# Storing q and k once, copying shifted keys inside SBUF, and moving value rows with GpSimd

## What is computed

```python
qkv = x @ W_attn + b_attn
q, k, v = heads(split(qkv))                    # 16 heads, 16 channels each
scores = einsum('bhtd,bhsd->bhts', q, k) * scale
mask = causal & (j >= i - 64)                  # each token sees itself and the 64 before it
attn = softmax(where(mask, scores, -inf))
x = layernorm(x + (attn @ v).reshape(b, t, c) @ W_proj + b_proj)
expert_idx = argmax(softmax(x @ Wr.T))
inter = sum_e (expert_idx == e) * gelu(x @ W1[e] + b1[e])
out = layernorm(x + layernorm(inter @ Wo + bo + x) * gamma + beta)
```

## Time and profile before

| | |
|---|---|
| median of three runs | 532.12 us (528.19 to 534.21) |
| the profiled execution | 528.38 us, of which its span is 526.7 us |
| mean granted TensorE clock | 0.979 of full speed |
| share of the span busy | PE 93%, DVE 82%, ACT 68%, POOL 60% |
| bytes moved by DMA | 80.96 MB |

### The profile page before, as it was taken

One profiled execution on the slowest core, in us unless ns is written; L12 is line 12 of the kernel. 1 busy time (PEld: TensorE's weight loads), 2 busy tenths in 40 slices (PEclk: granted clock), 3 DMA queues, 4 the chain that ended last, 5 costly groups with the idle time before them and its releaser, 6 DMA issues. The chain is left out here.

```text
span 526.7 us, 24512 instructions
## 1 busy us (share of the span) xinstructions
PE 489.4 (93%) x8574; PEld 432.2 (82%) x8574; DVE 431.5 (82%) x1132; ACT 356.5 (68%) x796; POOL 315.4 (60%) x553
## 2 busy tenths in 40 slices
PE   6989999999999999899978898999999999999980
PEld 5878888788888888688866787888999989999970
DVE  6558798878987898669898567999999989999983
ACT  5677778777876878467867664566667757666860
POOL 8612446444464545434634347777888878888883
PEclk9999999999999999989999898999999999999996
DMA  8687688786977797768772122222235554442200
GB/s 200 165 245 198 185 220 205 204 217 180 259 211 213 196 255 197 188 191 222 174 205 72 44 61 62 71 64 63 77 105 183 206 182 162 163 147 71 53 25 7
DMA packets 90184, 80.96 MB, mean 154 GB/s; under 512 B 36502, under 2 KB 83871, under 8 KB 90018
## 3 DMA queue, kind: packets, MB, share of 16 engines
q1 hardware_dynamic: 86720, 70.95, 48.9%
q0 software_dynamic: 3248, 8.41, 4.7%
q10 hardware_dynamic: 98, 0.04, 0.0%
HBM read 43.50 MB, written 23.55 MB: 127 GB/s over the span
## 5 line engine op out<-in xcount | busy, mean ns | idle before, releaser
L1415 PE MATMUL ps<-v_even,w_hi 128*128 128x128 f16 x1024 | 142.1, 220 | 0.6 <-issue 0.3
L1397 PE MATMUL ps<-wo_hi,ks 128*128 128x256 f16 (+1 forms) x576 | 129.2, 274 | 6.4 <-DVE ks L1091 6.1
L834 ACT ACTIVATE probs<-ps,b1T 128x128 f32<-128x128 f32 (+1 forms) x312 | 85.8, 361 | 66.9 <-PE ps L1415 66.7
L1415 PE MATMUL ps<-v_even,w_lo 128*128 128x128 f16 x512 | 108.6, 220 | 0.1
L1415 PEld LDWEIGHTS ps<-v_even,w_hi 128*128 x1024 | 97.2, 98 | 3.4 <-issue 1.3
L1162 DVE TENSOR_REDUCE mx<-ps 128x4 bf16<-128x512 f32 x128 | 82.5, 682 | 3.7 <-PE ps L1466 2.5
L1397 PE MATMUL ps<-wo_lo,ks 128*128 128x256 f16 (+1 forms) x288 | 78.9, 274 | 0.0
L1091 DVE TENSOR_TENSOR ks<-probs,ks 128x512 f16<-128x512 f32 (+1 forms) x72 | 70.9, 985 | 5.9 <-ACT ks L841 5.6
L853 ACT ACTIVATE probs<-ps 128x512 f32<-128x512 f32 x128 | 69.5, 610 | 5.3 <-PE ps L1492 4.4
L1515 PE MATMUL ps<-v_odd,probs 128*64 128x17 f32 x1024 | 69.4, 210 | 2.0 <-issue 2.0
L744 POOL CAST att_hi<-att 128x256 f16<-128x256 f32 x27 | 10.7, 395 | 100.9 <-DVE att L1219 100.9
(11 more groups left out here) (248 smaller groups left out, 1283.3 us busy)
## 6 DMA issues: line engine op xcount, KB each, us to landing
qk_s<-qk_room SPq DMA_DIRECT2D x32, 256.0 KB, 2.7
w_in<-in_L_ffn_W_dram SPq DMA_DIRECT2D x16, 512.0 KB, 5.7
v_odd<-slots SPq DMA_DIRECT2D x64, 128.0 KB
qs<-qk_s SPq DMA_DIRECT2D x16, 384.0 KB
ks<-qk_s SPq DMA_DIRECT2D x16, 384.0 KB, 5.5
ks<-qk_s SPq DMA_DIRECT2D x32, 144.0 KB, 3.2
v_even<-v_odd SPq DMA_DIRECT2D x63, 68.0 KB, 3.1
qk_s<-qk_room SPq DMA_DIRECT2D x32, 128.0 KB, 2.7
```

Of the source, the lines that this page charges most:

```text
L834: last = nc.scalar.activation(g[1 - p][:, ic, n * w:(n + 1) * w], ps_h[1 - p][:, half, col + n * w:col + (n + 1) * w], ACT.Gelu, bias=b1T[ ...
L1397: ins = mm(ps_y[p][0:m], h[p][hs][:, ic, 0:m], wo[ws][:, ic, :], start=n == 0, stop=n == 3 * IC - 1)
L1415: up_ins = mm(ps_h[1 - p][:, half, col + m * w:col + (m + 1) * w], weights(ws, m, k, ic), sT[1 - p][ss][:, k, at], start=k + n == 0, stop= ...
```

## The change

The high and the low part of q and k are each stored once, as they lie in SBUF: two DMAs a pair in place of four (L548 after), 512 KB in place of 768. The query stack and `ks[:, 1]` are read by three DMAs each (L485 after), one for each term; both in `stacks_begin`. The window is no longer read from DRAM: in `stacks_end`, when `ks[:, 1]` has landed, two DMAs copy it inside SBUF, from the `ks[:, 1]` of this pair and of the pair before (L510, L512 after), and PE's step 0 waits for both. The first pair keeps the old way with its own DRAM tensor. The value rows are copied by POOL (L765, L769 after). The rows of a tile are sent in every pass at the place of the odd ones.

```diff
-    qk_s = nc.dram_tensor("qk_s", [2, TILES // 2, P, 3, CC, 2 * P], f16, kind="Internal").ap()
+    qk_0 = nc.dram_tensor("qk_0", [2, P, 3, CC, 2 * P], f16, kind="Internal").ap()
+    qk_s = nc.dram_tensor("qk_s", [2, TILES // 2, P, 2, CC, 2 * P], f16, kind="Internal").ap()
...
+            def stack(g, w, dst, landing):
+
+                for j in range(3):
+                    rows = dst[2 * j:ALIGNED:6]
+                    sp.dma_start(rows.rearrange("r (h m) n -> r h (m n)", m=CC),
+                                 qk_s[PARTS[w][j], g].rearrange("(h d) w m n -> w d h (m n)", d=HD)[w]).then_inc(landing, 16)
...
-                q, new = stack_sources(g)
-                sp.dma_start(qs[k][0:ALIGNED:2, :, :].rearrange("r (h m) n -> r h (m n)", m=CC),
-                             q.rearrange("r h m n -> r h (m n)")).then_inc(stack_ld[k], 16)
-                windows(g, 0, new, stack_ld[k])
+                if g == 0:
+                    first_stack(0, qs[0], stack_ld[0])
+                    first_window(0, stack_ld[0])
+                    return
+                stack(g, 0, qs[k], stack_ld[k])
+                if g > 1:
+                    sp.wait_ge(window_ld[1 - k], 16 * window_loads(g - 1))
+                stack(g, 1, ks[k][:, 1, :, :], second_ld[k])
...
-                windows(g, 1, new, chunk_ld[k])
-                sp.dma_start(ks[k][0:ALIGNED:2, 1, :, :].rearrange("r (h m) n -> r h (m n)", m=CC),
-                             new.rearrange("r h m n -> r h (m n)")).then_inc(second_ld[k], 16)
...
+                sp.wait_ge(second_ld[k], 16 * second_loads(g))
+                sp.dma_start(ks[k][0:ALIGNED:2, 0, :, BLK:2 * P], ks[k][0:ALIGNED:2, 1, :, 0:2 * P - BLK]).then_inc(window_ld[k], 16)
+                sp.wait_ge(second_ld[1 - k], 16 * second_loads(g - 1))
+                sp.dma_start(ks[k][0:ALIGNED:2, 0, :, 0:BLK], ks[1 - k][0:ALIGNED:2, 1, :, 2 * P - BLK:2 * P]).then_inc(window_ld[k], 16)
...
-                    sp.wait_ge(v_out, m + 1)
-                    wait(sp, pv_done, CC * (m - VRING + 1))
-                    sp.dma_start(v_even[m % VRING][BLK:P, :, :], v_odd[m % VRING][0:BLK, :, :])\
-                        .then_inc(vtop_ld[m % 2], 16)
...
+                        if g > 0:
+                            sp.dma_start(qk_s[part, g].rearrange("p w m n -> p (w m n)"),
+                                         qk[g % 2][part].rearrange("p w m n -> p (w m n)")).then_inc(qk_st[g % 2], 16)
...
-                if it % 2 == 1 and a_tile(it - 4):
+                m = it
+                if a_tile(m):
+
+                    pool.wait_ge(v_out, m + 1)
+                    wait(pool, pv_done, CC * (m - VRING + 1))
...
+                    if a_tile(m - 5):
+                        pool.wait_ge(disp_st[(m - 5) % ROWS], 16 * ((m - 5) // ROWS + 1))
+                    nc.gpsimd.tensor_copy(v_even[m % VRING][BLK:P, :, :], v_odd[m % VRING][0:BLK, :, :]).then_inc(v_half_moved, 1)
+                    if a_tile(m + 1):
+                        wait(pool, pv_done, CC * (m + 2 - VRING))
+                        pool.wait_ge(v_half_moved, m + 1)
+                        nc.gpsimd.tensor_copy(v_even[(m + 1) % VRING][0:BLK, :, :], v_odd[m % VRING][BLK:P, :, :]).then_inc(v_moved, 1)
+                        pool.wait_ge(v_moved, m + 1)
...
+                if a_tile(it - 4):
                     send_rows(it - 4)
...
-                if it % 2 == 0 and a_tile(it - 4):
-                    send_rows(it - 4)
...
                     if step == 0:
-                        pe.wait_ge(stack_ld[pair % 2], 16 * (pair // 2 + 1 + window_loads(pair)))
+                        pe.wait_ge(stack_ld[pair % 2], 16 * stack_loads(pair))
+                        if pair > 0:
+                            pe.wait_ge(window_ld[pair % 2], 16 * window_loads(pair))
```

More of the change, by code:

```diff
@@ L299, in attention_then_routed_ffn @@
         stack_ld = [sem(f"stack_ld{k}") for k in range(2)]
-        chunk_ld = [sem(f"chunk_ld{k}") for k in range(2)]
+        window_ld = [sem(f"window_ld{k}") for k in range(2)]
         second_ld = [sem(f"second_ld{k}") for k in range(2)]
-        vtop_ld = [sem(f"vtop_ld{k}") for k in range(2)]
-        vlow_ld = [sem(f"vlow_ld{k}") for k in range(2)]
+        v_moved, v_half_moved = sem("v_moved"), sem("v_half_moved")
         w1_ld = [sem(f"w1_ld{k}") for k in range(2)]
@@ L366, in unit, with transfers, qk_stores, stack_loads @@
             return step % CC, step // CC, 2 * (step % CC) + step // CC
+        def transfers(g, at_first, later):
+            return sum(later if n else at_first for n in range(g % 2, g + 1, 2))
+        def qk_stores(g):
+            return transfers(g, 4, 2)
+        def stack_loads(g):
+            return transfers(g, 2, 3)
         def window_loads(g):
-            return sum(1 + (n > 0) for n in range(g % 2, g + 1, 2))
+            return transfers(g, 1, 2)
+        def second_loads(g):
+            return transfers(g, 1, 3)
         def turned(it):
@@ L556, in values_done @@
                 sp.wait_ge(pv_done, CC * (t + 1))
-                wait(sp, vtop_ld[t % 2], 16 * (t // 2 + 1))
-                if a_tile(t + 1):
-                    sp.wait_ge(vlow_ld[(t + 1) % 2], 16 * ((t + 2) // 2))
+                sp.wait_ge(v_half_moved, t + 1)
+                sp.wait_ge(v_moved, min(t + 1, TILES - 1))
             values_done(TILES - 4)
@@ L908, in _ @@
                     wait(act, pv_done, CC * (m - VRING + 1))
[L909 to L910 removed]
+                    wait(act, v_moved, m - VRING + 1)
                     nc.scalar.activation(
@@ L928, in _ @@
                     act.wait_ge(qk_done, new + 1)
-                    wait(act, qk_st[new // 2 % 2], 16 * QK_STORES * (new // 4))
+                    wait(act, qk_st[new // 2 % 2], 16 * qk_stores(new // 2 - 2))
                     nc.scalar.activation(qk[new // 2 % 2][0][:, :, :, new % 2 * P:new % 2 * P + P].rearrange("p w m t -> p (w m) t"),
@@ L1284, in _ @@
                     dve.wait_ge(qkh_done, new + 1)
-                    wait(dve, qk_st[new // 2 % 2], 16 * QK_STORES * (new // 4))
+                    wait(dve, qk_st[new // 2 % 2], 16 * qk_stores(new // 2 - 2))
                     hi, lo = (qk[new // 2 % 2][s][:, :, :, new % 2 * P:new % 2 * P + P].rearrange("p w m t -> p (w m) t")
```

54 lines of the change are left out of this document (26 added, 28 removed).

## The result

The changed kernel took 539.03 us in the median of 20 runs (533.8 to 546.18), the kernel before 532.69 us in 20 runs beside them. The ratio is 1.012 (1.009 to 1.015): slower, where 526 us and a faster kernel were forecast.

What follows compares the result with a forecast made beforehand. PE's matmuls were taken to set the pace, leaving only its gaps and low clock to gain. 528.4 us - 3.6 (gaps and clock) + 1.0 (late pairs) = 525.8, forecast 526 us; own range 521 to 530, overall 519 to 540.

Steps and rivals of the forecast that it cites:

- Value rows on POOL: Two value copies a pass on POOL, 1.05 us for both, fit into its waits for DVE: cost 0.
- Rival 3: POOL late: copies of 1.0 us or more delay `att_hi`; at 1.5 us a copy +15 us, 540; chance 0.06.
- gain 3.6 us of 7.2: In the attention passes, lighter DMA gives back half of the 7.2 us PE lost to gaps and low clock.
- The first term: Three PE "issue" gaps before 264 us, 3.8 us together, read as instructions arriving late under DMA load.
- late pairs: Pairs with less time from query issue to scores, first ones included, make PE wait: 1.0 us in all.
- The second: Lower granted clock at 220 to 240 us, behind the largest gap: 3.4 us of full clock lost.
- Rival 1: PE's gaps do not hang on DMA load, so the time stays at 528 to 533 us; chance 0.30.
- the chain of a pair: From a pair's first store to its scores: window there at 14.2 of 15.9 us, so the copy costs nothing.
- Rival 2: Window late: PE waits at step 0 of every even pass; 535 to 547 us; chance 0.22.
- Bytes: SP's DMA traffic falls by 528 KB a pair, to about 72.5 MB in all; DMA share 0.80 to about 0.68.
- The range: Whole kernel, 519 (6.5 us of gaps gone) to 540 us (late window at 1.1 us a pair); about 0.2 outside.

Runs made afterwards that it cites:

- e1: Kernel before with value rows copied by POOL and sends at one place, q and k as before, first kind of chip: ratio 0.998 to before.
- e16: Kernel before with value rows copied by POOL and sends at one place, q and k as before, on a chip of the second kind: ratio 1.018.
- e5: Changed kernel with value rows moved by DMA again, sends at one place, second kind of chip: ratio 1.001 to before.
- e8: Changed kernel with the first pair's DRAM tensor declared twice as large, half used, first kind of chip: ratio 0.999 to before, median 527.7 us.
- e7: Changed kernel repeated unedited, second kind of chip: ratio 1.013 to before; profiled execution 536.94 us.
- e13: Changed kernel with the first pair's DRAM tensor declared twice as large, half used, second kind of chip: ratio 1.013 to before, median 537.6 us.
- e12: Changed kernel repeated unedited, on one second-kind chip beside three other runs: ratio 1.012 to before.
- e11: Changed kernel with the first two pairs stored and loaded in the old way, repeated with more rounds, first kind of chip: ratio 0.998 to before.
- e4: Changed kernel with the second pair of tiles too stored and loaded in the old way, first kind of chip: ratio 0.995 to before.
- e2: Kernel before with only the sends moved to one place, first kind of chip: ratio 0.999 to before.
- e14: Kernel before, unchanged, run for its trace on a chip of the second kind: ratio 1.003.
- e3: Kernel before with only the new q and k path; value rows by DMA and sends as before, first kind of chip: ratio 1.022.
- e18: Changed kernel with value rows by DMA and the first two pairs in the old way, sends at one place, second kind of chip: ratio 1.003 to before.
- e15: Changed kernel with the two DRAM tensors of q and k declared in the other order, second kind of chip: ratio 1.007 to before.
- e17: Changed kernel with the send ahead of POOL's value copies, which wait for it to land, second kind of chip: ratio 1.033 to before.

## Why the prediction was wrong

**Step "Value rows on POOL", cost 0: this failed, and with it the direction.** On the first kind of chip, from which the trace of before came, it held (e1 0.998). On the second the copies, with the send behind them, cost 1.8% (e16) and the whole change 1.2%. The copy itself was sized well (0.45 forecast, 0.41 in most rows). Two things were not. For both copies I allowed 1.05 us; they hold the send back by 2.0. POOL's wait for `att` fell from 75.0 us in 23 (e5) to 39.1 in 22 (e8) and 35.1 in 22 (e7) between 60 and 260 us, so `att_hi` still had cover, as the forecast said. But I asked only what is late behind POOL's copies among POOL's own results, and not what the send does to others at its new time. Rival 3 was the wrong mishap of POOL: it needed a copy of 1.0 us and made `att_lo` late at once. In e7 `att_lo` is late too, 1.9 us in 5, but as a consequence: ahead of each of the five DVE waited 0.8 to 1.1 us for the product with v (L1548), then came `att`, then the split, then PE's transposes, which feed the next pass.

The size, by the same program on two chips: the medians of e8 and e13 are 527.7 and 537.6 us, 9.9 apart, of which the kernel before beside them has 3.5 (528.6 and 532.0). In the 22 passes e8 took 190.5 us, but 10.2 of them, from 177.6 us on, at the lower clock level, which is 5.1 us of full clock; without it 185.4, where e13 took 191.9, 6.5 us more. So the 22 passes show two thirds of the difference. The rest lies outside them, and I can't ascribe it. It isn't the clock dip at the end of the attention, which comes and goes on both kinds: first 266 to 274 us of e12 (second kind), then of e11 (first kind), columns as in the earlier trace rows.

```profile
266.00:274.00 8.00, 6.14 (x117) 4.61 (x116) 7.63 (x22) 4.00 (x7) 3.68 (x10) 0.79 0.50 167
266.00:274.00 8.00, 8.00 (x128) 7.01 (x129) 5.64 (x17) 4.31 (x8) 2.93 (x6) 0.50 0.57 140
```

**Step "gain 3.6 us of 7.2": too large.** Even where the results come at once, the ratio was 0.995 to 0.999 (e4, e8, e11), 0.5 to 2.5 us. Its two terms did not fare alike. The first term is the gaps. PE's idle time put down to "issue" between 60 and 260 us was 3.3 us before, and 2.7 and 3.0 in e1 and e2, which have the same q and k path. It was 3.4 in e8, 1.1 in e4 and 2.3 in e11, but of these 2.8, 0.5 and 1.7 stand ahead of score products, where PE waits for keys and windows; 0.6 is left in each. So on this kind of chip the gaps did become shorter, by about 2 us, and late pairs took part of it back. They are not pure chance either: the one of 1.34 us at 105.55 us comes back in pass 9 with 0.97 us in e1 and 0.56 in e4, e8 and e11, and not at all in e2 and e14. That the DMA load makes them is not shown. The second is the clock. The dip behind the gap at 222 us was real, but it belongs to one execution: e1, e2 and e14 have a mean clock of 1.00 from 60 to 260 us, and e8, with fewer bytes, 0.97. I counted 3.4 us of it as something that the kernel pays each time. Rival 1 was right in its outcome on these chips (the time of before), not in saying that the gaps stay.

**Step "the chain of a pair", 14.2 us of 15.9: right, with less to spare.** SP's issues for one pair in e8, then PE's first score product of that pair:

```profile
108.47 1.32 SPq L548 DMA_DIRECT2D qk_s<-qk_room  x2
111.54 2.76 SPq L485 DMA_DIRECT2D qs<-qk_s  x3
114.34 1.88 SPq L485 DMA_DIRECT2D ks<-qk_s  x3
...
118.59 0.59 SPq L510 DMA_DIRECT2D ks<-ks  x1
119.23 0.67 SPq L512 DMA_DIRECT2D ks<-ks  x1
...
124.34 0.41 PE L1500 MATMUL ps<-ks,qs 112*64 112x128 f16 x8
```

Queries 3.1 us after the first store (3.9 forecast), keys there at 10.1 (9.9 to 10.1), last window copy issued at 10.8. All L512 of e8:

```profile
DMA to landing us min/median/max: 3.5/4.3/6.1
```

I had 3.5, the shortest. This one landed after 3.9: 14.7 us in all, 1.2 to spare. The estimate from the Trainium skill, *DMA: Bandwidth & Descriptors*, anatomy of one DMA, of 2.2 to 2.9 us was further off still: no L512 of e8 landed in under 3.5 us. Late pairs cost 2.8 us in e8 between 60 and 260 us (PE's waits at L1500) and 0 to 1.1 in the changed kernel on chips of the second kind; forecast 1.0. Rival 2 decided in e3 alone, for a reason that stays open. That the POOL copies made room for the path is not shown: e5 and e18, with the value DMAs on SP's queue, had waits of 2.4 and 1.3 us there. The ends of the chain were also too near: by its own rows, the longest store landing (6.0) puts the queries at 7.2 and the window at 22.1 us, not 20.1, and the short ends give 10.9, not 11.9.

**Bytes: right, partly by luck,** 72.64 MB (72.5 forecast). The sum given, 80.96 less 15 x 0.528, is 73.0; what went is 15 x 256 KB of q and k and all 63 value copies of 68 KB, 8.3 MB. The share fell further than forecast, to 0.60 in e7 in place of 0.68. The longer passes are a part of it: e4 and e11 had 0.63 and 0.64 from 60 to 260 us. The value rows are the other part: with them still on the DMA queues, e5 and e18 had 0.69.

**The range.** Its lower end, 519, does not follow from 6.5 us of gaps gone, which gives 521.9, and the upper one, 540, should have been 541. The measured median stands near that end, but not for the reason the range was drawn there (rival 2).

**What I had not weighed at all** is that the profile of before came from a chip on which results are given on at once, and the trace of the changed kernel from one on which they are not. Little in the one trace could have shown it: 8 late results of 472.

## What to carry to other kernels

When work is put on an engine that also issues transfers, follow the transfer to its new time and look at what the other engines do there, not only at whether the engine itself has room. Before a cause is read from two sets of runs, see that one chip ran both: an identical program gave 0.999 on one chip and 1.013 on another, and that looked like the doing of an edit that did nothing. Compare medians of passes, not one stretch of one trace: a single clock dip in e8 hid 5.1 us. A single gap with its clock dip in one execution is not yet a cost of the kernel.

## What the runs showed of the hardware

On four of the six chips of the experiments (those of e5 to e7, of e12 to e15, of e16 and e17, and of e18), and in the profile of the changed kernel, an engine that waits for PE often starts late, by up to 1.3 us, if PE's result falls into a GpSimd send or shortly behind it (25 to 57 results in a trace). On the chips of e1 to e4 and e8 to e11, and in the trace of before, this is rare (1 to 8). It does not belong to the program: e8 and e13, and e1 and e16, are the same. What stays open is whether it belongs to the chip or to something else that lasts for one group of runs, and what holds the results back: PE's signal, or PE itself, whose product with v stands 0.3 to 0.4 us there in most cases (1.1 at the longest, e16). No kernel without the sends was run, and the sends at one place were not run without the new q and k path on a chip of the second kind.
